# Where a bias sum, an edge scaling and a routing chain stand in a four-layer convolution and expert kernel

## What is computed

```python
def cond(x, c):                          # TYPES = same, upsample, same, downsample
    for i, typ in enumerate(TYPES):
        s = c @ mod_w[i].T + mod_b[i]                     # one factor for each channel in
        weight = SCALE * w[i] * s[:, None, :, None]
        weight *= rsqrt(sum(weight ** 2, axis=(2, 3)) + EPS)[:, :, None, None]
        x = conv(x, weight, typ) + b[i]                   # up and down with a 4-tap blur
    return x

x = x + fp8_linear(cond(x, c))                            # layer 0
x = x + base(h) + sum over the top 2 of 16 experts of combine * (h @ A.T) @ B[e].T   # layer 1
x = x + base(h) + sum over e of sparsemax(h @ Wr + br)[e] * (h @ lora_A[e]) @ lora_B[e]  # layer 2
x = x + (silu(gate) * up) @ U2 @ V2 + b2,  gate, up = split((h @ U1) @ V1 + b1)      # layer 3
```

## Time and profile before

| | us |
|---|---|
| median of three runs | 2088.21 |
| lowest, highest | 2084.89, 2093.34 |
| the profiled execution | 2086.61 |
| its span (first to last instruction) | 2084.2 |

### The profile page before, as it was taken

One profiled execution on the slowest core, in us unless ns is written; L12 is line 12 of the kernel. 1 busy time (PEld: TensorE's weight loads), 2 busy tenths in 40 slices (PEclk: granted clock), 3 DMA queues, 4 the chain that ended last, 5 costly groups with the idle time before them and its releaser, 6 DMA issues. The chain is left out here.

```text
span 2084.2 us, 32136 instructions
## 1 busy us (share of the span) xinstructions
PE 1959.1 (94%) x10201; PEld 1663.0 (80%) x10209; DVE 1295.7 (62%) x2328; ACT 960.2 (46%) x1547; POOL 380.2 (18%) x457
## 2 busy tenths in 40 slices
PE   4799978799999989998899999988999999999999
PEld 4688834799999878886788888877888878878886
DVE  6888799777767764337667667666555444444443
ACT  4488755455555431114344444434666544433442
POOL 4122212211111100002111111112121223322331
PEclk9899999999999999999999999999999999999999
DMA  7566656311122165434221221123333211142114
GB/s 192 168 191 200 178 198 227 101 60 60 60 83 68 51 192 157 141 121 161 64 69 54 69 68 59 56 81 107 101 101 102 90 46 46 52 146 85 48 45 165
DMA packets 118609, 222.30 MB, mean 107 GB/s; under 512 B 18337, under 2 KB 65185, under 8 KB 117793
## 3 DMA queue, kind: packets, MB, share of 16 engines
q1 hardware_dynamic: 102048, 212.36, 32.5%
q10 hardware_dynamic: 16512, 9.31, 1.7%
HBM read 159.04 MB, written 62.59 MB: 106 GB/s over the span
## 5 line engine op out<-in xcount | busy, mean ns | idle before, releaser
L2701 DVE SCALAR_TENSOR_TENSOR f_prod<-ps,b,f_gate 128x512 f32<-128x512 f32 (+1 forms) x88 | 66.0, 750 | 160.3 <-ACT f_gate L2641 160.3
L125 POOL TENSOR_TENSOR rows<-l_EY,ones 128x4 f32<-128x4 f32 x128 | 32.2, 252 | 730.4 <-ACT rows L1360 365.4
L2742 POOL TENSOR_TENSOR x_lo<-f_prod,x_hi 128x512 fp32r<-128x512 f32 (+1 forms) x88 | 113.7, 1292 | 277.9 <-ACT x_hi L2648 277.9
L2571 PE MATMUL ps<-pt_hi,v_hi 128*128 128x512 f32 (+1 forms) x352 | 137.5, 391 | 1.7 <-PEq L644 1.7
L2571 PE MATMUL ps<-pt_lo,v_hi 128*128 128x512 f32 (+1 forms) x352 | 137.3, 390 | 0.0
L2571 PE MATMUL ps<-pt_hi,v_lo 128*128 128x512 f32 (+1 forms) x352 | 137.2, 390 | 0.0
L2641 ACT ACTIVATE f_gate<-ps,b 128x512 f32<-128x512 f32 (+1 forms) x88 | 60.5, 687 | 155.8 <-PE ps L2571 155.8
L1583 DVE SCALAR_TENSOR_TENSOR rows<-ps,dem3e,l_middle 128x512 f32<-128x512 f32 x60 | 45.1, 751 | 120.5 <-ACT l_middle L1329 97.7
L1097 PE MATMUL ps<-l_u_hi,l_g_hi 128*128 128x512 f32 x272 | 111.7, 411 | 5.9 <-DVE l_g_lo L1617 5.7
L125 POOL TENSOR_TENSOR XE<-rows,ones 128x8 f32 (+1 forms) x96 | 21.9, 250 | 511.4 <-DVE rows L1793 254.3
L1097 PE MATMUL ps<-l_u_lo,l_g_hi 128*128 128x512 f32 x272 | 108.7, 400 | 0.0
(11 more groups left out here) (408 smaller groups left out, 5800.1 us busy)
## 6 DMA issues: line engine op xcount, KB each, us to landing
x<-rows SPq DMA_DIRECT2D x64, 512.0 KB, 2.9
xin<-x SPq DMA_DIRECT2D x96, 256.0 KB, 4.0
rows<-x SPq DMA_DIRECT2D x48, 512.0 KB, 4.1
out<-rows SPq DMA_DIRECT2D x32, 512.0 KB, 2.6
v<-in_ffn_v SPq DMA_DIRECT2D x84, 128.0 KB, 2.6
xin<-in_x SPq DMA_DIRECT2D x16, 512.0 KB, 5.9
xb<-in_x SPq DMA_DIRECT2D x16, 512.0 KB, 3.3
x<-xb SPq DMA_DIRECT2D x16, 512.0 KB, 2.6
```

The source lines that it names most:

```text
L2571: mm = nc.tensor.matmul(ps[0:m, 2 * g + gu, :], v1sp[ws][:, s, r, gu, 0:m], pt[ms][:, r, cols], start=(k == 0), stop=(k == 5))
L2701: v.scalar_tensor_tensor(prod[0:m, g, :], ps[0:m, 2 * g + 1, :], b1[0:m, 1, bass.ds(2 * i + g, 1)], gate[0:m, g, :], ALU.add, ALU.mult).th ...
L2742: nc.gpsimd.tensor_tensor(asp[1][0:m, g, :], prod[0:m, g, :], asp[0][0:m, g, :].bitcast(F32), ALU.subtract).then_inc(al_ready, 1)
```

## The change

Six edits, all in the order of instructions and in where an intermediate result lies. No matmul and no DMA is added or removed.

1. `edges_u`, `edges_p`, `edges_v` on DVE: the product with the scale is written back into the bank it came from, and the term is added out of the bank. Before, the product went to SBUF and the addition read two SBUF tensors.
2. POOL's third chunk (k = 2, layers 1 and 2) waits for `pe_ready`, the end of `edges_p`.
3. POOL's bias addition of pair p waits for `sums_ready`, at `sum_c(p + 1)`, in layers 1 and 2 wherever a pair follows.
4. First pair of layers 1 and 2, DVE: `lead(1, 3)` is written out in the order differ_u, read_u_fast, read_a, split_z, split_x. In layer 2, `gates(0)` comes behind `sum_c(1)`, and the split of its transpose (`split_gt(0)`) comes right behind `differ_u(1)` on DVE and behind `read_u_fast(1)` on ACT, where it was in `tail(0)`.
5. Layer 1: in `tail(p)` the addition to banks 5 and 6 comes first, then the copy of the logits and the addition of bank 7. PE's `weights_g` waits for the first of these (`x_part`), not for the last.
6. Layer 1: `route` is cut into three. `route_largest(p)` stands at the end of `tail(p)`, `route_shares(p - 1)` between the two halves of `join_h(p)`, with ACT's `route_exp(p - 1)` behind its first `read_middle(p)`, and `route_pick(p - 1)` behind `split_h(p)`.

```diff
@@ PE, weights_g
-                    pe.wait_ge(xo_ready, r0 + p - 1)
+                    pe.wait_ge(x_part if layer == 1 else xo_ready, r0 + p - 1)
@@ ACT, first_pair
                     split_gc(1)
-                    lead(1, 3)
+                    read_u_fast(1)
+                    if layer == 2:
+                        split_gt(0)
+                    read_a(2)
+                    split_z(3)
+                    split_gaps(1)
+                    split_x(2)
@@ ACT, iteration
                 (read_middle if fast else read_h)(p, 0)
+                if layer == 1:
+                    route_exp(nc, act, kept, p - 1, sem)
@@ DVE, edges_p (edges_u and edges_v in the same way)
-                        step(v.tensor_tensor(f4, src, outer2(a2e[rows, own], 3, PW), ALU.mult))
-                        step(v.tensor_tensor(f4, f4, outer2(be2e[rows, own], 3, PW), ALU.add))
+                        step(v.tensor_tensor(src, src, outer2(a2e[rows, own], 3, PW), ALU.mult))
+                        step(v.tensor_tensor(f4, src, outer2(be2e[rows, own], 3, PW), ALU.add))
@@ DVE, tail
                 if layer == 1:
-                    if not (isinstance(p, int) and p == 0):
-                        route(nc, dve, kept, p - 1, sem)
                     dve.wait_ge(ffn_done, r0 + p + 1)
-                    v.tensor_copy(kept["small"][:, :], ps[:, 7, REST:THIRD]).then_inc(small_read, 1)
...
                     v.tensor_tensor(x2, ps[:, 5:7, 0:THIRD].rearrange("p c (m s) -> p s c m", s=2), x2,
                                     ALU.add).then_inc(x_part, 1)
+                    v.tensor_copy(kept["small"][:, :], ps[:, 7, REST:THIRD]).then_inc(small_read, 1)
...
+                    route_largest(nc, dve, kept, p, sem)
                     return
@@ DVE, first_pair
-                        if layer == 2:
-                            gates(0)
                         if layer > 1:
                             wait_lo(dve, len(chunks) - 1)
                         sum_c(1)
+                        if layer == 2:
+                            gates(0)
                     split_g(1)
...
-                        lead(1, 3)
+                        differ_u(1)
+                        if layer == 2:
+                            split_gt(0)
+                        read_u_fast(1)
+                        read_a(2)
+                        split_z(3)
+                        split_x(2)
@@ DVE, iteration
                     join_h(p, 0)
+                    if layer == 1:
+                        route_shares(nc, dve, kept, p - 1, sem)
...
                     join_h(p, 1)
...
                 split_h(p)
+                if layer == 1:
+                    route_pick(nc, dve, kept, p - 1, sem)
@@ POOL
             for k in range(min(POOL_CHUNKS, len(chunks))):
+                if k == 2:
+                    pool.wait_ge(pe_ready, n)
                 chunk(k)
...
                 if with_ffn:
+                    if ahead:
+                        pool.wait_ge(sums_ready, 2 * (f0 + p) + 3)
                     pool.wait_ge(xr_loaded, 16 * (r0 + p + 1))
                     g.tensor_tensor(xr[:, :], xr[:, :], bias[:, :], ALU.add).then_inc(xr_biased, 1)
```

More of the change, by code:

```diff
@@ L1378, in tail @@
             def tail(p):
-                if layer == 1 and not (isinstance(p, int) and p == 0):
-                    route_exp(nc, act, kept, p - 1, sem)
-                if layer == 2:
-                    act.wait_ge(side[1], side0[1] + p + 1)
-                    nc.scalar.activation(gsp[0][:, :], ps[:, 7, 3 * P:4 * P], ACT.Copy).then_inc(side[2], 1)
+                if layer == 2 and not (isinstance(p, int) and p == 0):
+                    split_gt(p)
                 if layer == 3:
@@ L2032, in carry @@
         v.memset(carrier[:, j:j + 1], 0.0)
-    dve.wait_ge(sem("small_read"), p + 1)
-    carry(0)
-    link(0, v.max(top[:, :], small[:, R1:R1 + E1]))
-    v.tensor_copy(kept["res"][:, bass.ds(p, 1), :], small[:, 0:R1].unsqueeze(1))
-    v.tensor_scalar(nmax[:, :], top[:, 0:1], -1.0, None, ALU.mult).then_inc(nmax_ready, 1)
     dve.wait_ge(ex_ready, p + 1)
@@ L2049, in route, with route_pick, link @@
     link(8, v.reciprocal(den[:, 1:2], den[:, 1:2]))
+def route_pick(nc, dve, kept, p, sem):
+    v = nc.vector
+    links = sem("r_links")
+    iota, top, ex, prob, indexf, den, pick = (kept[k] for k in ("iota", "top", "ex", "prob", "indexf", "den", "pick"))
+    def link(j, ins):
+        ins.then_inc(links, 1)
+        dve.wait_ge(links, ROUTE_LINKS * p + j + 1)
     link(9, v.tensor_scalar(pick[:, :], top[:, 0:2], den[:, 1:2], 0.5, ALU.mult, ALU.mult))
@@ L2446, in _ @@
             lo(1, 1)
-            route(nc, dve, kept, NP - 1, sem)
+            route_shares(nc, dve, kept, NP - 1, sem)
+            route_pick(nc, dve, kept, NP - 1, sem)
             lo(2, 0)
```

43 lines of the change are left out of this document (28 added, 15 removed).

## The result

| | before | changed |
|---|---|---|
| median of the runs, us | 2086.55 (4 runs, 2078.55 to 2093.34) | 2050.03 (4 runs, 2048.38 to 2052.03) |
| profiled execution: time, span | 2086.6, 2084.2 | 2048.45, 2046.5 |
| ratio, estimated from all runs | | 0.984 (95% interval 0.980 to 0.988) |

What follows compares the result with a forecast made beforehand. PE bounds the kernel, busy 1959.1 of 2084.2 us; only its idle time and the clock can change. 7.7 + 4.9 + 16.1 + 2.2 = 30.9 off 2086.6 gives 2055.7, median 2057.3; range 2045 to 2071.

Steps and rivals of the forecast that it cites:

- Part A: Edges of layers 1 to 3 (edits 1, 2): additions out of PSUM escape POOL's hold; 7.7 us less (3 to 12).
- Part B: End of first pairs, layers 1 and 2 (edits 4, 3): earlier sum shortens PE's waits; 4.9 us less (1 to 10).
- Part C: Later pairs, layers 1 and 2 (edit 3): POOL's bias addition no longer holds sum_c; 16.1 us less (9 to 18).
- Part D: Layer 1's routing (edits 5, 6): weights_g no longer waits behind 13 links; 2.2 us less (-4 to 3).
- R1: Stalls move: PE's new waits call half-clock stretches, POOL holds DVE elsewhere; 17 to 18 us less, about 2070; chance 0.22.
- R2: Stalls vanish whole, no half-clock stretch left in the first pairs; 43 us less, 2045; chance 0.14.
- R3: Layer 1's links between the joins delay PE; slower, 2099 if the links take 6.4 us; chance 0.03.
- R4: POOL isn't what holds these DVE operations, edits 1 to 3 cure nothing; 7 us less, 2081; chance 0.06.

Runs made afterwards that it cites:

- The further version: The changed kernel with POOL's third chunk waiting for the end of edges_v and DVE's first own chunk moved behind edges_v: 2043.51 us, ratio 0.9831.
- The four parts alone: The kernel before with edit 1, edit 3, edit 4, or edits 5 and 6 alone: 2071.95, 2066.72, 2076.51 and 2073.96 us.

## Why the prediction was right, and where it wasn't

- **Part A, right.** Forecast 7.7. Additions at 0.46 us, both starts in layer 1 met within 0.1 us, layer 2's L1021 3.5 us earlier than its stage's start (3.4 forecast), layer 3's 3.1 (2.8). The two new stalls brought 6.8 us of half clock each, and 1.1 and 1.2 were given back by the time `ffn` ran, not 0.8; 0.6 and 0.5 of that show as a longer wait of `ffn` for H's low part (1.59 and 1.51 us instead of 0.99 and 0.98). Edit 1 alone gives 8.0 by the trace; that edit 2 adds to it was wrong. The estimate from the Trainium skill (VectorE: DVE Perf Modes, the trn2 errata), 1.8 us more for sources in a bank, isn't borne out: 455 ns against 449 at best in SBUF, and writing into the bank costs 10 ns.
- **Part B, right in sum, in part by luck, and wrong in its working.** Forecast 4.9, alone 5.3 by the medians. By the trace edit 4 alone gives 3.3 in layer 2's first pair and loses 2.1 in layer 1; the rest is that two pairs of layer 2 are held and not four. `weights_g` of layer 2's first pair gains 3.4 us on the product ahead of it in the pair (L1077 at 980 in the trace of before), as forecast, and the clock takes nothing off. But L1205 waits for 0.55 and not 2.2. I let POOL's bias addition hold L1612 for the 2.1 us that the earlier sum gives; in the changed kernel it starts at 978.20, 2.7 us ahead of L1621, falls on one operation of `gates` (L1766, a wait of 0.8 for PE at L1191 behind it), and L1621 is free. That is luck as well: without edit 2 the addition starts at 977.01 and falls on L1621, and L1205 waits for 1.6. The further version shows the same case, the one that I had forecast: held, 1.8 us at L1205. L1116's new wait of 1.9 came as forecast. In layer 1 the gain is edit 3's; edit 4 alone costs 2 us there.
- **Part C, right.** Forecast 16.1, alone 15, taken from the change 12. In the middle pairs of layers 1 and 2 no wait of PE for H's low part is left. That fewer pairs happened to be hit without edit 3 (two in layer 2 and none in layer 1 behind the first) fits the 12.
- **Part D, the step that failed.** Forecast 2.2; the waits of L1077 gave 5.5 in the changed kernel between 434 and 714 alone, and 6.3 over the 13 pairs with edits 5 and 6 alone. The mechanism was right (PE no longer waits behind the links; the joins aren't late). The term was mis-sized: I took the idle time that the view of waits shows (3.0) for what a wait costs, and took off 0.8 for costs of which 0.25 came (lost in the last pair in all nine profiles with edit 6 and in none of the five without it). Start to start it was 5.2 us in the trace of before, there to be read.
- **The clock.** My terms held 4.8 us for it, net (6.0 in C and 0.8 in layer 1's B, less 1.6 in A and 0.4 in B). The time at half clock fell by 24.2 us, which at half speed is up to 12. Two differences belong to no edit as far as the profiles show: the stretch at 1437 us in layer 3 (1.5 us of layer 3's surplus) stands in the profile of before and in that of edit 5 alone, and in no other, whichever edits it has; that at the start of the experts (748, -1.1 us) is absent in the profile of before and in five runs of this study, and 3.4 or 6.8 us long in eight.
- **The rivals.** R1's mechanism was seen (waits at L1021 with 6.8 us at half clock behind them) but not its size. Of R2 one part came, L1621 unheld; the clock did not, with 6.8 us at half clock in the first pairs of layers 1 and 2. R3 and R4 fell. The links between the joins take 1.7 us (1.8 forecast), and in the same pair as above the second join still waits 1.07 us for ACT:
```profile
589.76 0.16 DVE L2082 RECIPROCAL den<-den 128x1 f32<-128x1 f32 x1
591.00 0.75 DVE L1592 SCALAR_TENSOR_TENSOR rows<-ps,dem3e,l_middle 128x512 f32<-128x512 f32 x1 [1.07 <-ACT l_middle L1329]
```
Edits 1 and 3, each alone, brought what R4 gave to them as zero. The four parts alone sum to 38 us, against medians of 2081 to 2082 for the kernel before; together they gave 31.9 against 2080.49 on one chip. So they overlap by some 6 us. The traces offer a reason: edits 4, 5 and 6, alone, had two held pairs fewer in layer 2, which edit 3 frees in any case. That this is the whole overlap isn't shown.

## What to carry to other kernels

Read what a short wait costs from start to start against the pitch without a wait, not from the idle column; in a loop the difference counts each time. Where DVE and POOL share SBUF, give each long POOL operation a stretch of DVE work that reads a bank, and wait for the event that begins it. When such a hold is removed, look at the next operation with SBUF sources: here the hold fell on it, however small it was, and the edit that only shifted it gave nothing. Compare parts and whole against the same baseline: the kernel before alone gave medians from 2080 to 2087.

## What was not expected of the hardware

The hold isn't confined to operations with two SBUF tensors. A TENSOR_SCALAR of 128x2 elements, which reads one tensor and its scalar from SBUF, is held too; which of its accesses is the cause isn't shown. L2095 in the changed kernel meets POOL's bias addition in 15 of 16 pairs (ns min/median/max):
```profile
L2095 DVE TENSOR_SCALAR pick<-top,den x16: 229/1326/2131, 411.9 to 767.5; 128x2 f32<-128x2 f32 x16
```
It costs nothing, since DVE waits for PE behind it (2.12 us above). In the same profile L1559 (a bank, a scalar and a tensor from SBUF) ran four times under POOL's third chunks and took 473 to 484 ns, and L1633 (a bank and a tensor) 29 times beside POOL's bias additions, 1.22 to 1.23 us: none was held. And POOL waits as well: in the run with 973.80 above, its addition started 0.12 us after DVE's and took 2.89 us instead of 2.42. This agrees with what the Trainium skill says (SBUF — State Buffer, Who interferes with whom), that the one that starts second waits.
